# One post-norm attention and feed-forward layer on one core: the value products' waits moved inside the output product, the lower-half flag from a product with ones, loads and weight splits reordered

## What is computed

```python
q = (x @ Wq.T + bq).reshape(B, S, H, D)      # H = 16, D = 32
k = (x @ Wk.T + bk).reshape(B, S, H, D)
v = (x @ Wv.T + bv).reshape(B, S, H, D)
q, k = rotate(q, cos, sin), rotate(k, cos, sin)
att = softmax(einsum('bshd,bstd->bsht', q, k) / sqrt(D), axis=-1)
out = einsum('bsht,bstd->bshd', att, v)
out = swapaxes(out, 1, 2).reshape(B, S, E)
x = layernorm(x + out @ Wo.T + bo)
g, u = (x @ gate_w.T) * gate_s, (x @ up_w.T) * up_s
x = layernorm(x + ((silu(g) * u) @ down_w.T) * down_s)
```

## Time and profile before

| | |
|---|---|
| median of 3 executions | 1951.37 us (1948.12 to 1951.77) |
| the profiled execution | 1946.58 us |
| its span, first to last instruction | 1944.8 us |
| TensorE busy | 1835.3 us, 94% |
| VectorE busy | 1188.0 us, 61% |
| ScalarE / GpSimd busy | 714.1 us, 37% / 740.4 us, 38% |
| mean granted TensorE clock | 0.984 |

### The profile page before, as it was taken

The page is one execution under the profiler, slowest core; times in us unless marked ns, Lnnn a source line. Parts: engine busy times, 40 slices in busy tenths (PEclk is TensorE's granted clock), DMA queues, the critical chain, the costliest instruction groups (busy, mean ns, idle before and its releaser), DMA issues.

```text
span 1944.8 us, 41042 instructions
## 1 busy us (share of the span) xinstructions
PE 1835.3 (94%) x15488; PEld 1474.9 (76%) x15488; DVE 1188.0 (61%) x1734; ACT 714.1 (37%) x1138; POOL 740.4 (38%) x571
## 2 busy tenths in 40 slices
PE   6899999999999999996599999999999999999997
PEld 5677777777777777775488888888888888888885
DVE  6688888888888888886234444344443444434443
ACT  4444555445544545443222222222222222222221
POOL 5676777777877777673010111001110011101111
PEclk9999999999999999998799999999999999999998
DMA  6346555665566645665601112011110111101011
GB/s 196 102 122 166 140 138 138 163 165 131 135 148 165 145 137 137 160 181 143 223 13 64 57 42 65 33 65 38 59 65 32 65 38 59 65 32 65 33 32 43
DMA packets 257790, 194.47 MB, mean 100 GB/s; under 512 B 143056, under 2 KB 182608, under 8 KB 257744
## 3 DMA queue, kind: packets, MB, share of 16 engines
q1 hardware_dynamic: 257744, 193.84, 36.2%
HBM read 109.13 MB, written 84.67 MB: 100 GB/s over the span
## 4 chain that ended last, share of the span: by engine, by line
PE 41%; issue 9%; POOL 1%; DVE 0%; DMA 0%; ACT 0%; POOLq 0%; DVEq 0%; SPq 0%; ACTq 0%
PE ps_g L829 7%; PE ps_g L826 7%; PE ps_u L826 7%; PE ps_u L829 7%; PE acc L846 7%; PE acc L843 7%; POOL z L909 1%; DMA dscale<-down_s 0%; DVE xT_lo L978 0%; DVE z L958 0%; POOL rs L911 0%; POOLq L698 0%; DVE hid L926 0%; ACT act_g L876 0%; DVE z L940 0%
## 5 line engine op out<-in xcount | busy, mean ns | idle before, releaser
L926 DVE SCALAR_TENSOR_TENSOR hid<-ps_u,gu_scale,act_g 128x512 f32<-128x512 f32 x176 | 132.1, 751 | 450.7 <-ACT act_g L876 450.7
L909 POOL TENSOR_TENSOR z<-z,wide 128x512 f32<-128x512 f32 x64 | 80.7, 1293 | 731.0 <-DVE z L940 731.0
L876 ACT ACTIVATE act_g<-ps_g,gu_scale 128x512 f32<-128x512 f32 x176 | 121.4, 690 | 574.3 <-PE ps_u L829 574.3
L324 PE MATMUL ps_x<-w_hi,xc_hi 128*128 128x512 f32 x768 | 309.1, 402 | 17.3 <-POOL xc_lo L477 7.9
L325 PE MATMUL ps_x<-w_lo,xc_hi 128*128 128x512 f32 x768 | 305.3, 398 | 0.0
L326 PE MATMUL ps_x<-w_hi,xc_lo 128*128 128x512 f32 x768 | 305.0, 397 | 0.0
L497 POOL TENSOR_TENSOR qk_cos<-qk_in,rot 128x512 f32<-128x512 f32 x128 | 204.1, 1595 | 165.7 <-DVE qk_in L572 141.3
L843 PE MATMUL acc<-wf_rest,hid_hi 128*128 128x512 f32 x640 | 252.6, 395 | 1.2 <-DVE hid_lo L932 1.2
L829 PE MATMUL ps_g<-xT_lo,wf_rest 128*128 128x512 f32 x640 | 253.2, 396 | 0.0
L846 PE MATMUL acc<-wf_rest,hid_lo 128*128 128x512 f32 x640 | 252.8, 395 | 0.0
L826 PE MATMUL ps_u<-xT_hi,wf_rest 128*128 128x512 f32 x640 | 252.6, 395 | 0.0
(11 more groups left out here) (85 smaller groups left out, 2955.6 us busy)
## 6 DMA issues: line engine op xcount, KB each, us to landing
xc<-x_cols SPq DMA_DIRECT2D x32, 512.0 KB, 4.4
v_rows<-v_in SPq DMA_DIRECT2D x32, 512.0 KB, 3.2
v<-v_rows SPq DMA_DIRECT2D x32, 512.0 KB, 5.5
res<-x_rows SPq DMA_DIRECT2D x64, 256.0 KB, 2.9
x_rows<-x_out SPq DMA_DIRECT2D x32, 512.0 KB, 3.3
x_cols<-x_turn SPq DMA_DIRECT2D x128, 128.0 KB, 2.4
wide<-x_rows SPq DMA_DIRECT2D x16, 1024.0 KB, 5.5
out<-z SPq DMA_DIRECT2D x64, 256.0 KB, 3.1
```

The source lines that it names most:

```text
L324: pe.matmul(out, hi[:, k], w_hi[:, w, k], start=(k == 0), stop=False)
L926: dve.scalar_tensor_tensor(out=hid[:, :], in0=slot(u, j)[1][:, :], scalar=gu_scale[:, 1, j:j + 1], in1=act_g[:, :], op0=ALU.mult, op1=ALU. ...
```

## The change

Three edits.

First, in the loop `inputs_of_av` is called inside `project`, ahead of the last of the twelve matmuls of tile 1's output projection.

Second, the flag: in step 33 VectorE reduces `lo_top`, TensorE multiplies the 128x1 result with a column of ones into one element of `ps_x0`, and VectorE compares that element with zero at once. The `partition_all_reduce` on GpSimd is gone.

Third, the start: SyncE loads K, the tables, K's bias, Q, Q's bias, V, V's bias, and in step 1 the identity, O and O's bias, each constant with a semaphore of its own. VectorE splits K, rearranges the tables, splits Q; V is split in step 1 after the first sines of Q, and O and the mask at the end of step 1. ScalarE splits O at the end of step 1.

```diff
@@ SyncE
+            load_weights(1)
+            sp.dma_start(qT[:, 0]..., rope...).then_inc(rope_loaded, 16)
+            load_bias(1)
+            load_weights(0)
+            load_bias(0)
+            load_weights(2)
+            load_bias(2)
             sp.wait_ge(halves_made, 2)
...
             def step(s):
...
+                if isinstance(s, int) and s == 1:
+                    sp.dma_start(ident[:, :], eye).then_inc(eye_loaded, 16)
+                    load_weights(3)
+                    load_bias(3)
@@ TensorE
-            def project(out, hi, lo, w, sem_done, first_use):
+            def project(out, hi, lo, w, sem_done, first_use, next_av=None):
...
                     pe.matmul(out, hi[:, k], w_lo[:, w, k], start=False, stop=False)
+                    if k == KE - 1 and next_av is not None:
+                        inputs_of_av(next_av)
                     last = pe.matmul(out, lo[:, k], w_hi[:, w, k], start=False, stop=(k == KE - 1))
...
-                        if t == 1 and not isinstance(s, int):
-                            inputs_of_av(s - 2)
                         project(ps_x[2 + t][:, :], aT_hi[:, t], aT_lo[:, t], 3, o_done,
-                                isinstance(m, int) and m == 0 and t == 0)
+                                isinstance(m, int) and m == 0 and t == 0,
+                                next_av=s - 2 if t == 1 and not isinstance(s, int) else None)
...
+                if isinstance(s, int) and s == UNITS + 1:
+                    pe.wait_ge(lo_reduced, 1)
+                    pe.matmul(ps_x[0][0:1, 0:1], lo_top1[:, :], ones[:, :], start=True, stop=True).then_inc(lo_joined, 1)
@@ ScalarE
-            for w in W_ORDER:
+            def high_weights(w):
...
+            for w in W_ORDER[:3]:
+                high_weights(w)
...
                     spread_k(m, 1)
+                    if isinstance(m, int) and m == 0:
+                        high_weights(3)
@@ GpSimd
-            pool.wait_ge(const_loaded, 16 * 6)
-            for w in range(2):
+            for w in W_ORDER[:2]:
+                pool.wait_ge(bias_loaded[w], 16)
                 pool.tensor_copy(*of_kind(w, bias[:, w], bias_raw[:, w])).then_inc(bias_made, 1)
...
-                if isinstance(s, int) and s == UNITS + 2:
-                    pool.wait_ge(lo_reduced, 1)
-                    pool.partition_all_reduce(lo_top1[:, 1:2], lo_top1[:, 0:1], P, bass.bass_isa.ReduceOp.max)\
-                        .then_inc(lo_joined, 1)
@@ VectorE
+            low_weights(1)
+            dve.wait_ge(rope_loaded, 16)
...
+            low_weights(0)
...
                     sines(m, 0, 0)
+                    if isinstance(m, int) and m == 0:
+                        low_weights(2)
...
                     add_bias(m, 1, 2)
+                    if isinstance(m, int) and m == 0:
+                        low_weights(3)
+                        dve.wait_ge(eye_loaded, 16)
+                        dve.tensor_reduce(own4[:, :], ident[:, :].rearrange("p (r j k) -> p j r k", r=2, j=A4), AX.XY,
+                                          ALU.max).then_inc(own_made, 1)
...
-                if isinstance(s, int) and s == UNITS + 2:
+                if isinstance(s, int) and s == UNITS + 1:
                     dve.wait_ge(lo_seen, SLABS)
-                    dve.tensor_reduce(lo_top1[:, 0:1], lo_top[:, :], AX.X, ALU.max).then_inc(lo_reduced, 1)
+                    dve.tensor_reduce(lo_top1[:, :], lo_top[:, :], AX.X, ALU.max).then_inc(lo_reduced, 1)
+                    dve.wait_ge(lo_joined, 1)
+                    dve.tensor_scalar(shared.inexact[0:1, :], ps_x[0][0:1, 0:1], 0.0, None, ALU.is_gt)\
+                       .then_inc(flag_set, 1)
```

More of the change, by code:

```diff
@@ L199, in attention_phase @@
         lo_top = sb("lo_top", [P, SLABS])
-        lo_top1 = sb("lo_top1", [P, 2])
+        lo_top1 = sb("lo_top1", [P, 1])
+        ones = sb("ones", [P, 1])
         ps_x = [ctx.enter_context(nc.psum_tensor(f"ps_x{b}", [P, E], F32)) for b in range(4)]
@@ L239, in _, with load_weights @@
         def _(sp):
-            for w in W_ORDER:
+            def load_weights(w):
                 at = W_ORDER.index(w)
@@ L248, in _, with load_bias @@
                         sp.dma_start(xc[:, :], x_cols2[0]).then_inc(xc_loaded, 16)
-                if at == 1:
-                    for b in range(4):
-                        sp.dma_start(bias_raw[:, b] if b < 2 else bias[:, b], biases[b:b + 1, :].to_broadcast([P, E]))\
-                          .then_inc(const_loaded, 16)
-                    sp.dma_start(ident[:, :], eye).then_inc(const_loaded, 16)
-                    sp.dma_start(qT[:, 0].rearrange("p h i -> p (h i)").rearrange("p (g x) -> p g x", g=2 * ROPES),
-                                 rope.rearrange("g p w d -> p g (w d)")).then_inc(const_loaded, 16)
+            def load_bias(w):
+                sp.dma_start(bias_raw[:, w] if w < 2 else bias[:, w], biases[w:w + 1, :].to_broadcast([P, E]))\
+                  .then_inc(bias_loaded[w], 16)
+            load_weights(1)
+            sp.dma_start(qT[:, 0].rearrange("p h i -> p (h i)").rearrange("p (g x) -> p g x", g=2 * ROPES),
+                         rope.rearrange("g p w d -> p g (w d)")).then_inc(rope_loaded, 16)
+            load_bias(1)
[3 more added lines that the diff above has]
+            load_bias(2)
             sp.wait_ge(halves_made, 2)
@@ L542, in _, with low_weights @@
             dve.memset(ps_s[:, :, :], 0.0).then_inc(idle_cleared, 1)
-            for w in W_ORDER:
+            def low_weights(w):
                 at = W_ORDER.index(w)
```

32 lines of the change are left out of this document (17 added, 15 removed).

## The result

| | before | after |
|---|---|---|
| median, us | 1950.33 (4 runs, 1948.12 to 1951.77) | 1915.37 (4 runs, 1915.03 to 1916.99) |
| ratio of the medians, 95% interval | | 0.9823 [0.9806, 0.984] |
| profiled execution, us | 1946.58 | 1915.49 |
| span, us | 1944.8 | 1913.7 |
| TensorE busy, us | 1835.3, 94% | 1835.0, 96% |

The change takes 35.0 us, where 36.1 was forecast from a median that stood 1 us higher (1951.37). The time, 1915.37, lies on the forecast of 1915.3. TensorE does the same work; what went is idle time. Whether each term was right is another question, since errors can cancel.

A forecast was written before the change was run, and what follows sets the result against it. TensorE works nearly all the time, so only its idle time can be won. Loop 25.4, flag 7.8 and start 2.9 sum to 36.1 us, taking the 1951.4 us median to 1915.3; range 1910 to 1924.

The forecast's parts named there:

- The loop: Tile 1's output projection: moving the waits eleven matmuls on removes a 0.94 us stall in 27 turns, 25.4 us.
- rival 1: Loop: the waits cost a gap at their new place, loop gain only 17.8 us, 1922.9 us in all; chance 0.14.
- The flag: Between the phases: without the all-reduce, `var_eps` follows `mean_var` at once, 7.8 us gained, bounds 6.6 and 7.9.
- The start: Loads and splits reordered: tables come earlier, second half of the first scores starts 2.9 us earlier; bounds 0 and 3.7.
- four (2.7 us) now stand ahead of the third: Start, VectorE: four weight splits, priced at 2.7 us, now precede the third bias; eight (5.36 us) leave the first.
- to about 38: Start: O's splits hold VectorE to about 38 us, so `top` starts only 1.3 us earlier than before.
- The range: Whole kernel: 1910 to 1922 us from the forecast's own bounds and run spread, widened to 1924 to hold two rivals.
- The offset: Whole kernel: the median lay 4.8 us above the profiled 1946.58; this distance was carried to the changed kernel.
- The waits cost a gap: Loop: waits between matmuls of a stream leave a gap, total gain 28.5 us, 1922.9 us; chance 0.14.
- The short products starve: Loop's short-matmul bursts: a 1.98 us stop each turn loses 53.5 us, 17.4 slower, 1968.8 us; chance 0.02.
- The start loses: Start: tables as late as before, V projection and first scores 2 to 3 us later, 1920.7 us; chance 0.13.
- The stall is not `pX`: Loop: the stall is the wait for Q's bias, so the loop gives nothing, 1940.7 us; chance 0.03.

The follow-up runs named there:

- e5: Changed kernel with the loop's waits ahead of the third matmul of tile 1's output projection instead of the twelfth; 1926.12 us, ratio 0.9879 to the kernel before.
- e1: Kernel before with the first edit alone (the wait moved inside the output projection); 1925.61 us against 1951.88, ratio 0.9862.
- e2: Kernel before with the second edit alone (flag from a product with ones in step 33); 1943.79 us, ratio 0.9954.
- e9: Changed kernel with GpSimd's all-reduce in step 34 instead of the product with ones, VectorE's reduction in step 33; 1918.27 us, ratio 0.9827 to the kernel before.
- e4: Kernel before with no edit, run and profiled again; 1950.47 us, ratio 0.9997.

## Why the prediction was right, point by point

**The loop, 25.4 forecast, 26 to 27 measured.** Right in mechanism, somewhat small. The first matmul after a stall took 0.07 us more, show 0.47 against 0.40; I had taken this refill as the upper bound only. It is real (in the kernel before the next start came 0.31 us later, at 503.07, instead of 0.23, and e5's stop shows the same): the turn went from 27.28 to 26.28, 1.00 and not 0.94. From the beginning of step 6 to the value products of step 32, 26 turns, four profiles of the old loop show 731.7 to 731.8 us and nine of the new one 705.4 to 706.3: 26.1. With a 27th turn like them that is 27.1, and e1 gives 26.3 in the median. The prices of zero for the waits (rival 1) held: the spacing at the new place is the usual one.

**The flag, 7.8 forecast, 7.6 measured by the traces, 8.1 by e2.** Right. The Trainium skill, GPSIMD Engine Reference, section Instruction dispatch, gave about 6 us for a first call to freshly loaded code, and e9 shows 5.77 us of "issue" ahead of the all-reduce: the trace agrees with it in size there. But there is a second gap, behind it, of 7.11 to 7.51 us in three kernels, and it is this one that stood on the path. I had read the 6 us as a smaller measure of this gap; the runs show two gaps. That the second is the return to other GpSimd code is argued from its place, not shown: it follows the all-reduce wherever that is put, and GpSimd's list has a further instruction (`ISA`) directly ahead of the reduction (L535) and another directly behind it (L510), one at each gap.

**The start, 2.9 forecast, about 2.3 by whole times (1.4 to 5.1), 0.2 to 0.8 by the traces.** The size lies in the interval, the working does not hold, so as far as it was met it was luck. The step that failed is "four (2.7 us) now stand ahead of the third": I priced the splits by a row in which GpSimd stood idle, and moved them beside its rotations. They took 5.75 us, and V's projection waited for them three times. With that the second K spread came at 33.87 and not 31.9, and the second half of the scores at 36.56 instead of 37.49, 0.9 earlier instead of 2.9. The rearrangement of the tables, which now stands ahead of Q's splits, had no price in the sum and cost 2.23 us there. O's splits, "to about 38", ended at 41.3, so that `top` started at 41.41, 2 us later than before, where 1.3 earlier was forecast. The tables came better than forecast, 19.64 against 20.7.

Why the whole times still show a gain of 2.3 us is open. Behind the first scores, steps 2 to 4 run for some microseconds at the 1.2 GHz level, longer in one execution and shorter in another (step 3 begins at 67.0 and at 70.1 in the same program), and an early gain of 1 us cannot be followed through this in single profiles. The sum of the three parts measured alone, 26.3 + 8.1 + 2.3 = 36.7, is 1.7 above the 35.0 of all together, within the spread. By the traces the loop (27.1) and the flag (7.6) alone make 34.7 of the 35.0, which would leave little for the start: then the total of 36.1 came so near because the loop gave 1.7 more than its term and the start less.

**The range.** One of its sums does not come out. With the lowest term of each part, 17.8, 6.6 and 0, the gain is 24.4 and the time 1927.0, above the 1924 at which the range ends.

**The offset.** The distance of 4.8 us between profile and median was carried on. Taking the median as the base was right, since the first profile was a favourable one, as e4 shows. The same sentence of the prediction had the profile of the changed kernel at 1910.5; it came at 1915.49, at its own median, so the distance belongs to the execution and not to profiling. Whoever had trusted the two profiles, 1946.58 and 1915.49, would have seen 31.1 us.

**The rivals.** *The waits cost a gap*: refuted at its new place: 0.24 us from the eleventh matmul (492.30) to the twelfth (492.54), 0.33 from there to the burst, as before. The loss of a pulled-ahead weight load, which the Trainium skill (TensorE: Matmul & The Clock Gate, Architectural detail) would let one expect, does not show in these distances. *The short products starve*: refuted, 1.48 us and no "issue" in the loop's bursts; the program stops only in the written-out steps, five times, 9.9 us (9.1 to 12.1 in the other profiles). The 1.80 us of the first value products, which this rival took as a sign, went with the clock, which fell during them (in e4 it fell before them, and they took 2.05; in the changed kernel behind them, and they took 1.48). The Trainium skill, Runtime: NRT & Kernel Launch, section Instruction fetch mechanics, has the crossing into new code mostly hidden. That the five stops are such crossings was my reading; no run here shows what they are. *The start loses*: half true in the trace (V's projection waited 2.1 us in three pieces for its low parts, `top` was late), not in the time. *The stall is not `pX`*: refuted by e1, and by e5, in which a stop for the same input comes back in part when the waits come nearer to it.

## What to carry to other kernels

A wait belongs directly ahead of the first instruction that reads what it guards; one that stood twelve matmuls ahead of it cost 1 us in each of 27 turns, and moved eleven matmuls on it cost nothing. A price taken from a row holds only beside the neighbours of that row: a split took 0.62 us with GpSimd idle and 1.44 beside it. And before comparing one profile with another, compare each with the median of its kernel, and with a second profile stage by stage: two executions of one program stood 4.1 us apart at the beginning of step 6, some 3 of them from one stretch at the lower clock and what follows it.

## What the runs showed of the hardware

- A subtraction of two 128x512 inputs on VectorE took 0.62 us with GpSimd idle, 1.44 on average beside GpSimd's rotations and 1.03 beside `xc_lo` and `f_lo` (twice: 4.13 and 4.10 for four). The sines, which have two such inputs as well, took 0.65 to 0.69 us where they began ahead of GpSimd's operation and 1.06 to 1.11 where one was running, and these ended 0.54 to 0.56 us after it (GpSimd to 26.14, 32.01 and, after the change, 21.49 us; the sines to 26.70, 32.56 and 22.03): they look held until it ends. The biases (0.68), which read a bank of TensorE's, did not grow.
- A cross-partition reduction of one column on GpSimd is 0.38 us of work with 5.77 us ahead of it and 7.11 to 7.51 behind it; the same question put to TensorE is 0.19 us.
- After TensorE had waited 3.2 us, the granted clock fell to the 1.2 GHz level, in two profiles 0.8 and 1.6 us into the burst of short products, in one about a microsecond ahead of it. It came back between 64 and 74 us, at different times in executions of one program (between 64 and 66 and between 72 and 74).
